# Second attention on Trainium2: the weighing of values placed behind the fourth head of a group, the division of the output one slot part later

## What is computed

```python
Q = einsum('bsh,nhd->bnsd', x, Wq) + bq      # 8 heads of 32
qq, kq = Q @ Wc2q + bc2q, K @ Wc2q + bc2q     # 8 numbers per head and row
fid = einsum('bnsq,bntq->bnst', qq, kq) / max(|qq| |kq|, 1e-8)
qw = fid * (1.0 + 0.1 * sin(fid * pi))
cw = einsum('bnsd,bntd->bnst', Q, K) / sqrt(32)
probs = softmax(0.5 * qw + 0.5 * cw)
attn = einsum('bnst,bntd->bnsd', probs, V)   -> 512 x 256, @ Wo + bo
x1 = layernorm(x + attn, g1, beta1)
out = layernorm(x1 + small_ffn(x1), g2, beta2)
```

## Time and profile before

| | |
|---|---|
| median of three runs | 3728.39 us |
| the profiled execution, its own time | 3728.92 us |
| its span | 3727.1 us |
| mean granted TensorE clock | 0.922 |
| TensorE busy | 3135.2 us, 84% |
| VectorE busy | 2741.7 us, 74% |
| ScalarE busy | 2198.9 us, 59% |
| GpSimd busy | 1114.8 us, 30% |

### The profile page before, as it was taken

The page is one execution under the profiler, slowest core; times in us unless marked ns, Lnnn a source line. Parts: engine busy times, 40 slices in busy tenths (PEclk is TensorE's granted clock), DMA queues, the critical chain, the costliest instruction groups (busy, mean ns, idle before and its releaser), DMA issues. The chain is left out here.

```text
span 3727.1 us, 70608 instructions
## 1 busy us (share of the span) xinstructions
PE 3135.2 (84%) x24024; PEld 2426.1 (65%) x24024; DVE 2741.7 (74%) x7223; ACT 2198.9 (59%) x5352; POOL 1114.8 (30%) x658
## 2 busy tenths in 40 slices
PE   6899898998991899997488888888888886499998
PEld 4666666666661799886265655556655554488888
DVE  4676676766765898992378878877887885599996
ACT  4666676676671344441377777777777775244443
POOL 1000000000000555551233433334343333355554
PEclk9999999999995999998699999999999997799999
DMA  5244343442421000001343434444343442211100
GB/s 88 43 67 60 48 72 50 62 65 43 61 37 63 6 18 18 18 18 67 48 55 55 72 58 69 63 71 67 58 69 63 64 62 40 74 35 35 35 29 23
DMA packets 134182, 190.46 MB, mean 51 GB/s; under 512 B 15126, under 2 KB 81558, under 8 KB 133142
## 3 DMA queue, kind: packets, MB, share of 16 engines
q1 hardware_dynamic: 133830, 185.95, 29.6%
HBM read 45.65 MB, written 28.84 MB: 20 GB/s over the span
## 5 line engine op out<-in xcount | busy, mean ns | idle before, releaser
L408 ACT ACTIVATE a_probs<-a_probs,a_negmax 128x176 f32<-128x176 f32 (+4 forms) x1024 | 501.6, 490 | 333.7 <-DVE a_negmax L331 333.3
L331 DVE CUSTOM_DVE_ANT_0 a_probs<-a_mask,a_score 128x176 f32<-128x176 f32 (+4 forms) x1024 | 403.8, 400 | 224.7 <-PE a_score L482 96.4
L493 PE MATMUL a_turned<-ident,a_probs 128*128 128x128 f32 (+1 forms) x2176 | 430.0, 290 | 77.8 <-DVE a_pT L340 70.9
L1765 ACT ACTIVATE b_u<-b_u,b_negmax 128x512 f32<-128x512 f32 x512 | 366.3, 716 | 98.2 <-DVE b_negmax L1645 97.7
L1645 DVE CUSTOM_DVE_ANT_0 b_u<-b_u,b_score 128x512 f32<-128x512 f32 x512 | 340.0, 681 | 101.5 <-PE b_score L1891 100.5
L1091 PE MATMUL f_y_bank<-f_wdT,f_hqT 128*128 128x256 f32 x1536 | 358.7, 383 | 44.6 <-DVE xs L964 42.5
L1900 PE MATMUL b_turned<-ident,b_u 128*128 128x128 f32 x2048 | 334.7, 290 | 72.8 <-DVE b_pT L1651 44.2
L1637 DVE SCALAR_TENSOR_TENSOR b_u<-b_u,b_score 128x1024 f32<-128x1024 f32 x256 | 309.1, 1214 | 90.8 <-ACT b_u L1758 88.9
L1758 ACT ACTIVATE b_u<-b_score 128x1024 f32<-128x1024 f32 x256 | 262.2, 1024 | 156.9 <-PE b_score L1881 156.6
L1900 PEld LDWEIGHTS b_turned<-ident,b_u 128*128 128x128 f32 x2048 | 250.4, 148 | 159.1 <-issue 124.1
L1091 PEld LDWEIGHTS f_y_bank<-f_wdT,f_hqT 128*128 128x128 f32 x1536 | 284.6, 190 | 92.6 <-DVE xs L964 55.0
(11 more groups left out here) (233 smaller groups left out, 7022.6 us busy)
## 6 DMA issues: line engine op xcount, KB each, us to landing
b_stack<-b_part SPq DMA_DIRECT2D x192, 256.0 KB, 8.3
a_stack_q<-a_part SPq DMA_DIRECT2D x192, 128.0 KB, 4.3
a_stack_k<-a_part SPq DMA_DIRECT2D x192, 128.0 KB, 5.8
xs<-in_x_dram SPq DMA_DIRECT2D x16, 512.0 KB, 8.4
x_before_b<-xs SPq DMA_DIRECT2D x16, 512.0 KB, 2.9
b_xin<-x_before_b SPq DMA_DIRECT2D x16, 512.0 KB, 12.3
b_xres<-x_before_b SPq DMA_DIRECT2D x16, 512.0 KB, 3.9
x_after_b<-b_xres SPq DMA_DIRECT2D x16, 512.0 KB, 2.9
```

The source lines that it names most:

```text
L331: dve.tensor_tensor_reduce(out=probs[:, n % 2, j, 0:keys(n)], in0=mask_of(n), in1=score[j][:, 0:keys(n)], scale=-1.0, scalar=3.0e38, op0=A ...
L408: act.activation(probs[:, n % 2, j, 0:keys(n)], probs[:, n % 2, j, 0:keys(n)], ACT.Exp, bias=negmax[:, n, j:j + 1], scale=-1.0, accum_out= ...
L493: m = nc.tensor.transpose(turned[j % 2][0:rows, u, :], chunk(n, probs[:, n % 2, j, :], u), ident[:])
L1765: act.activation(u[:, n, j, :], u[:, n, j, :], ACT.Exp, bias=negmax[:, n, j:j + 1], scale=-1.0, accum_out=sums[:, c, t, j:j + 1]).then_inc ...
```

## The change

`weigh` moves on TensorE from part 1 to part 3 of its slot, behind the transposes of the fourth head. `move_out` moves on VectorE from (5, 1) to (6, 0) and from (9, 3) to (10, 0).

```diff
-                        if (n, j) in ((5, 1), (9, 3)) and has(s):
+                        if (n, j) in ((6, 0), (10, 0)) and has(s):
                             move_out(s, n // 8)
...
-                        if has(s) and j == 1 and 2 <= n <= B_GROUPS + 1:
+                        if has(s) and j == 3 and 2 <= n <= B_GROUPS + 1:
                             weigh(s, n - 2)
```

## The result

The changed kernel takes 3761.52 us, median of seven runs (3751.01 to 3766.76), against 3728.39 for the kernel before (seven runs, 3723.77 to 3740.59): ratio 1.0082, 95% interval 1.0067 to 1.0098. It is 33 us slower where 9 us faster was forecast, and outside the range given. The span of its profiled execution is 3765.0 us against 3727.1, its mean granted TensorE clock 0.914 against 0.922.

The account below looks back on a forecast made before the run. No full engine but short handovers between engines were taken to hold slots 1 to 8. Of 2.87 us won per body, 0.69 remained, 0.6 as mean; times 16 gives 9.6 us, so 3719.3 us, range 3688 to 3752.

Parts of the forecast that it names:

- Part 1: Weighing behind head 3 in the second attention: side steps drop out of the handovers, slots 3 and 5 about 4.45 us each.
- the ring: Short handovers between engines holding slots 1 to 8, 4.82 us a turn, with weighing and side step both in it.
- Part 2: First division moved to slot 6, under side step m0: VectorE's idle 0.75 us goes, first sine 2.87 us earlier so far.
- the walk: Start times followed through the queues from the first transposes of slot 2, using traced intervals and 0.61 us per VectorE step.
- four small steps (1.2 us): VectorE in slot 6, between its last sum with maximum and the first of slot 7: taken as 1.2 us together.
- the 2.87 us won: Gain per body up to the first sine: from 2472.36 to 2469.49.
- Part 3: Late weighing of group 7 and second division, slots 9 and 10: gain given back, 0.69 of 2.87 us left at y0.
- the sum: Whole kernel: 16 sequences at a mean gain of 0.6 us give 9.6 us, 3728.92 to 3719.3 us.
- rival D: TensorE's granted clock falls before y0 in slot 10; lower case 3749 us, counted as slower; chance 0.10.
- Rival C: Slots 9 and 10 lose more than slots 2 to 8 win; with a gain of 0.7 us, 3753 us; chance 0.13.
- Rival B: Gain of slots 2 to 8 kept to the body's end: all of it 46 us, 3683 us; chance 0.33.
- Theory 1: From the follow-up, not the prediction: three costs add up, the small step's stall, the late end, the low clock behind new waits.

Follow-up runs that it names:

- both: The changed kernel with the late weighing and second division put back and the four small VectorE steps at (7, 3): 3676.88 us, ratio 0.9862 against the kernel before.

## Why the prediction was wrong

- **Part 1** (the side steps leave the ring, GpSimd's 10.53 us set the spread): right, to 0.03 us at two of its first points, and 0.35 us late at the first T of slot 6, because GpSimd starts 1.98 us before the first T of slot 2 here, not 2.32. Slots 3 and 5 took 4.44 and 4.48 us, forecast about 4.45.
- **Part 2** (division under m0, no wait for the reciprocals): the wait is gone. But the walk on to "four small steps (1.2 us)" is **the step that failed**. I took their durations from a body in which they came at the end of GpSimd's addition L1494. Counted from the first T of slot 2, they moved forward by 2.68 us (from 27.16 to 24.48) while that addition moved by 0.74 (25.26 to 24.52), so they fell into it. From the M ahead of them to the M behind them the trace has 3.49 us (2479.98 to 2483.47) instead of the 1.78 of the walk. The last M comes 30.40 us behind the first T of slot 2, forecast 28.49, before 31.36: the 2.87 us won shrink to 0.96. Taking the stall away is worth 29 us with the late end (1.0082 to 1.0005) and 36 us with the end as before (0.9959 to 0.9862).
- **Part 3** (the late end gives back 2.2 us): the mechanism holds. Dots to weighing took 0.53 us, within the bounds of 0.43 and 0.6; VectorE idled 0.51 us before the cosine term, where about 1 was forecast; y0 came 0.83 us behind the division. The size was too small: 2.2 us a sequence are 35 us, the end costs 1.2 to 1.4%, 46 to 53 us or about 3 us a sequence. The low clock comes with it, which the sum put at nothing and left to rival D: 29 us of the 46 are TensorE's wait before y0, 17 us are the slow y0.
- **Rival D** (the clock falls before y0) happened, in 12 of 16 sequences, with 3.50 us for 1.97 in the body above. It had a chance of 0.10, since the wait stands between busy stretches; that did not keep the clock up. The range takes in a lower case of D, 3749 us, with y0 at twice its 1.97 us in every sequence. No run shows that term, which was my estimate: the runs show 3.04 to 3.56 us in 12 sequences and 1.97 us in four. The rival was thought of in one place. In the changed kernel there are two (slots 7 and 10), and the late weighing alone brings a third (slot 9). Its case of y0 alone has no stall in it.
- **Rival C** (the head wins less than the end loses) happened too; its cause was not GpSimd's roots but GpSimd's addition. **Rival B**, 46 us, is near what the head brings once both obstacles are gone (52 us measured); its condition, that the late end costs little, was not met.

The terms are -1.4% for the head, +1.4% for the late end and +0.8% for the stall, which make +0.8%; they must, since each kernel differs from the next by one of them. The test is the other order: with the stall put in first it costs 1.0% and the end 1.2%, each within 0.2% of the first value. Theory 1's third cost, the low clock, is not a fixed term beside the other two: it sits in the slow y0 and in other places, and it moved (to V0, to slot 9) when a wait was taken away or filled. The changed kernel differs from that of "both" in two things: the place of the small steps, which the change never touched, and its own late end.

## What to carry to other kernels

When steps of one engine move in time, look at what runs beside every later step, also the small ones: a 0.18 us step took 2.26 us when another engine's instruction had just begun, and 0.18 us again once that instruction was moved. Price a wait of TensorE not only by its length but by what may run behind it at the low clock (here y0, 3.50 us at 0.54 behind a wait of 1.81, instead of 1.97), and take care before moving a step out of a wait that it filled: here such a wait grew from 0.46 to 1.50 us and cost 22 us in all. Edits that each lose alone (weighing 0.8%, division 0.4%) can win together, 1.4%, when each is the other's cause of waiting.

## What was not expected of the hardware

- A VectorE tensor_scalar on 128x32 numbers held for 2.25 us by a GpSimd tensor_tensor on 128x1024, in 13 of 16 sequences; 0.18 us in the median once that addition was moved.
- The granted clock of TensorE fell behind single waits of 1.24 us (late division alone: y0 took 3.65 us at 0.53), 1.50 (the late weighing at 0.52), 1.81 (y0 at 0.54) and 2.53 us (a weighing at 0.50) in a stretch that was otherwise busy. It stayed at 1.00 behind one of 2.54 us, to fall 20 us later in the same body (V0 at 0.54).
- Useless products in a wait made the kernel faster, 1.0005 to 0.998 with intervals apart; 1.0082 to 1.006, where the intervals still touch, points the same way.
